# The second mixture's collected head blocks, its last three blocks, shared tail copies and filler products

## The reference

```
x0   cross attention, 8 heads of 128          l1  rotated self attention
x1, x2  cross attention, 16 heads of 8        f2  causal attention, 16 heads of 8, with rotary embedding
m2   mixture of 8 experts on h (1024 x 128), two experts for each token:
     lg  = h @ router                          # 1024 x 8
     w   = softmax(top2(lg))                   # two weights a token, zero for the other experts
     out = sum_e w[:, e] * ((silu(h @ gate_e) * (h @ up_e)) @ down_e)   # hidden size 448
```

## Time and profile before

| | |
|---|---|
| median of 3 runs | 928.2 us (922.79 to 929.34) |
| profiled execution | 926.85 us, its span 925.0 us, so 1.85 us around it |
| PE, DVE, ACT, POOL busy | 861.3, 648.6, 574.3, 305.4 us |
| mean granted clock of PE | 0.988 |
| m2, from the logits to its last table product | 539.6 to 645.4 us of the span |
| chain that ended last, by engine | PE 69%, DVE 14%, ACT 10%, issue 4%, DMA 2% |

### The profile page before, as it was taken

How to read it: one execution, slowest core, us unless ns; L and a number is a source line. 1 busy time by engine, 2 the same in 40 slices (tenths; PEclk the granted TensorE clock), 3 DMA queues, 4 the chain that set the end, 5 groups by cost and what they waited for, 6 DMA issues and landing times.

```text
span 925.0 us, 14478 instructions
## 1 busy us (share of the span) xinstructions
PE 861.3 (93%) x4568; PEld 561.1 (61%) x4568; DVE 648.6 (70%) x1153; ACT 574.3 (62%) x1080; POOL 305.4 (33%) x297
## 2 busy tenths in 40 slices
PE   8999998999899887989899889999999999999997
PEld 4666645775545433535545546776357888888885
DVE  4666716777779578659578663542358999999996
ACT  5456614666557554478578631332677888888886
POOL 0111004764048300028348425435001333444430
PEclk9999999999999999999999999999999999999999
DMA  9000000111000000000000063203008999999882
GB/s 364 14 1 0 0 1 18 52 34 66 1 1 2 1 0 1 1 0 2 2 1 1 3 258 96 82 24 100 7 1 212 241 233 242 245 245 245 234 225 64
DMA packets 27744, 76.70 MB, mean 83 GB/s; under 512 B 4464, under 2 KB 10864, under 8 KB 27264
## 3 DMA queue, kind: packets, MB, share of 16 engines
q1 hardware_dynamic: 26448, 73.50, 28.9%
q0 software_dynamic: 1248, 2.57, 0.8%
HBM read 72.31 MB, written 5.27 MB: 84 GB/s over the span
## 4 chain that ended last, share of the span: by engine, by line
PE 69%; DVE 14%; ACT 10%; issue 4%; DMA 2%; SPq 0%; ACTq 0%; DVEq 0%
PE ps L802 9%; PE ps L804 9%; PE ps L803 9%; PE ps L592 4%; PE ps L1175 4%; PE ps L584 3%; PE ps L603 3%; PE ps L1191 2%; PE ps L219 2%; ACT arena L699 2%; ACT arena L1848 2%; PE ps L1453 2%; PE ps L1534 1%; PE ps L1486 1%; PE ps L1506 1%
## 5 line engine op out<-in xcount | busy, mean ns | idle before, releaser
L802 PE MATMUL ps<-parts 128*128 128x512 f32 x416 | 166.6, 401 | 3.7 <-DVE ps L2463 1.2
L804 PE MATMUL ps<-parts 128*128 128x512 f32 x416 | 162.1, 390 | 0.0
L803 PE MATMUL ps<-parts 128*128 128x512 f32 x416 | 161.9, 389 | 0.0
L832 ACT ACTIVATE parts<-ps 128x512 fp32r<-128x512 f32 x192 | 115.2, 600 | 53.1 <-PE ps L804 24.0
L836 DVE TENSOR_TENSOR parts<-ps,parts 128x512 fp32r<-128x512 f32 x192 | 132.5, 690 | 7.0 <-ACT parts L832 0.8
L820 POOL TENSOR_TENSOR parts<-ring,zeros 128x1024 fp32r<-128x1024 f32 (+2 forms) x36 | 51.1, 1420 | 178.7 <-PE ps L804 141.8
L2463 DVE TENSOR_TENSOR ps<-ps,arena 128x512 f32<-128x512 f32 x156 | 108.1, 693 | 2.7 <-DMA arena<-m_comb 1.8
L802 PEld LDWEIGHTS ps<-parts 128*128 128x128 f32 x416 | 78.2, 188 | 24.6 <-DVE parts L836 3.3
L1997 ACT ACTIVATE ps<-ps 128x512 f32<-128x512 f32 x156 | 90.8, 582 | 2.7 <-PE ps L804 0.4
L804 PEld LDWEIGHTS ps<-parts 128*128 128x128 f32 x416 | 78.1, 188 | 16.4
L803 PEld LDWEIGHTS ps<-parts 128*128 128x128 f32 x416 | 78.1, 188 | 16.2 <-issue 0.5
(11 more groups left out here) (460 smaller groups left out, 1517.8 us busy)
## 6 DMA issues: line engine op xcount, KB each, us to landing
arena<-m_comb SPq DMA_DIRECT2D x156, 256.0 KB, 5.5
ring<-m_in SPq DMA_DIRECT2D x20, 512.0 KB
arena<-m_in SPq DMA_DIRECT2D x4, 1408.0 KB
pack<-pack_in SPq DMA_DIRECT2D x1, 2058.5 KB, 10.6
ring<-m_up_in SPq DMA_DIRECT2D x8, 256.0 KB
slots_x<-empty_in SPq DMA_DIRECT2D x1, 1491.6 KB
pack<-pack_in SPq DMA_DIRECT2D x1, 1186.0 KB, 14.7
pack<-pack_in SPq DMA_DIRECT2D x1, 1149.5 KB, 12.4
```

The costliest lines, as they stand in the source:

```text
L802: nc.tensor.matmul(dst, w_high, x_high, start=start, stop=False, skip_group_check=True)
L803: nc.tensor.matmul(dst, w_high, x_low, start=False, stop=False, skip_group_check=True)
L804: return nc.tensor.matmul(dst, w_low, x_high, start=False, stop=stop, skip_group_check=True)
L832: nc.scalar.activation(m_hh[0:rows, p], ps[0:rows, src, :], ACT.Copy).then_inc(R(t, "_hh"), 1)
```

## The change

- m2's head: `SOON` goes from 6 to 8. The rows are rounded to `s_high` by ACT (an additional copy for each half), POOL subtracts to get `s_low`, and PE multiplies both with 0/1 matrices of 128 x 1024, all in the rounded type F32R: four products of 512 columns for each sequence. Their buffers now lie where `s_xs` is, so SP's row loads wait for the last of these products as well.
- Each row in `slots_x` carries the token's 8 routing weights too (`ROW` from 129 to 137 columns).
- m2's last 3 blocks (`LATE`) are not scattered. From their destinations DVE makes 0/1 matrices of 128 x 1024 (`late_weights` after block 16, `late_place` after blocks 17 to 19); ACT scales and rounds y (`s_yh`), DVE gets the rest (`s_yl`), and PE adds four products of 512 columns for each block to the result's banks, after the loop and ahead of the fills, which are 6 and not 28. Of these three blocks the middle one has bank 4 and not bank 7. The tables are loaded when 20 scatters have landed; the rows of the late pairs read as zero, since `slots_y` is zeroed by one DMA early in the program.
- Attention, last sequence: ACT copies bank 4 and DVE bank 5. Half 1 of the output product is cut in two, 384 columns that wait for 7 sequences and 128 that wait for the last.
- x0: `x_normalise(0, 0)` moves ahead of DVE's six small instructions, with 5 fills on PE ahead of the loop. l1: 6 fills between the two halves of a turn, and 18 where 13 were.
- POOL's `m3_split(0, 0)` waits for the last `down`.

The diff, without the buffers that only get another address and the list of semaphore counts:

```diff
@@ -38,7 +38,8 @@
-SOON = 6
+SOON = 8
+LATE = 3
...
@@ -77,10 +78,10 @@
-ROW = P + 1
+ROW = P + 1 + E
...
-LOADS = (SOON, SOON + 2, SOON + 6, SOON + 12, NB)
-FILL_COUNT, FILL_TABLE = 13, 28
+LOADS = (SOON, SOON + 2, SOON + 6, NB - LATE, NB)
+FILL_COUNT, FILL_TABLE = 13, 6
...
@@ -141,9 +142,17 @@
-        with ExitStack() as overlaid:
-            overlaid.enter_context(nc.sbuf_tensor("below_parts", [P, PARTS], F32))
-            parts = overlaid.enter_context(nc.sbuf_tensor("parts", [P, PARTS_COLS], F32R))
+        def rounded(name, lo, cols):
+
+            with ExitStack() as overlaid:
+                overlaid.enter_context(nc.sbuf_tensor("below_" + name, [P, lo], F32))
+                return overlaid.enter_context(nc.sbuf_tensor(name, [P, cols], F32R))
+
+        parts = rounded("parts", PARTS, PARTS_COLS)
+        places = [rounded(f"places_{b}", lo, SOON * P) for b, lo in enumerate((1408, 6528, 8576, 2432, 3456, 4480, 22912, 26128))]
+        late_places = [rounded("late_0", 24016, T), rounded("late_1", 25040, T), places[0]]
+        late_y = rounded("late_y", 448, 2 * LATE * P)
+        turned_high, turned_low = rounded("turned_high", 20864, T), rounded("turned_low", 21888, T)
...
@@ -588,6 +605,8 @@
                 wait("_pt", w)
+                if w == WAVES - 1:
+                    wait("_last", 1)
...
@@ -595,6 +614,8 @@
                 wait("_pt", 2 * b + 2)
+                if b == B - 1:
+                    wait("_last", 2)
...
@@ -649,9 +670,12 @@
                 residual_seed(pe)
-            for p in range(2):
-                wait("_oT", HB * (p + 1))
-                mm(bank(p), wo, half(a_oT, p), start=rope, stop=True, skip_group_check=True).then_inc(S(done), 1)
+            wait("_oT", HB)
+            mm(bank(0), wo, half(a_oT, 0), start=rope, stop=True, skip_group_check=True).then_inc(S(done), 1)
+            wait("_oT", B - 1)
+            mm(ps[:, 1, 0:HALF - P], wo, a_oT[:, HALF:T - P], start=rope, stop=False, skip_group_check=True)
+            wait("_oT", B)
+            mm(ps[:, 1, HALF - P:HALF], wo, a_oT[:, T - P:T], start=False, stop=True, skip_group_check=True).then_inc(S(done), 1)
...
@@ -696,6 +720,10 @@
                 wait("_turned", w + 1)
+                if b == B - 1:
+                    nc.scalar.activation(a_pt[:, b % 2, NH // 2 * v:NH // 2 * v + 4, :],
+                                         bank(4).rearrange("p (n q) -> p n q", n=4), ACT.Copy).then_inc(R(t, "_pt"), 1)
+                    return
...
@@ -773,8 +801,17 @@
                     inverse(b - 1)
-                if b >= 2:
+                if 2 <= b < B - 1:
                     outputs(b - 2)
+
+            def last_copies(v):
+                wait("_turned", WAVES - 1 + v)
+                nc.vector.tensor_copy(a_pt[:, (B - 1) % 2, NH // 2 * v + 4:NH // 2 * (v + 1), :],
+                                      bank(5).rearrange("p (n q) -> p n q", n=4)).then_inc(R(t, "_last"), 1)
+
+            last_copies(0)
+            outputs(B - 3)
+            last_copies(1)
...
@@ -1088,10 +1125,14 @@
             sp.dma_start(slots_x, empty_in).then_inc(R("m2", "_load1"), 16)
+            sp.wait_ge(S("filled"), 7)
+            sp.dma_start(slots_y[0:2 * T, :].rearrange("(p r c) f -> p r (c f)", p=P, c=2),
+                         zeros[:, :].bitcast(F32).unsqueeze(1).to_broadcast([P, 2 * T // P // 2, 2 * P])).then_inc(R("m2", "_load1"), 16)
...
             sp.wait_ge(S("s_scattered"), 16 * 2 * B)
+            waits(sp, "m2")("_xwl", 2)
...
@@ -1099,7 +1140,7 @@
         def sorted_tables(sp):
-            sp.wait_ge(S("s_out"), 16 * NB)
+            sp.wait_ge(S("s_out"), 16 * (NB - LATE))
...
@@ -1109,6 +1150,12 @@
+        def late(j):
+            return NB - LATE <= j < NB
+
+        def y_bank(j):
+            return 4 if late(j) and (j - (NB - LATE)) % 2 else 7
+
...
@@ -1119,15 +1166,19 @@
             nc.gpsimd.iota(s_dest[:, :, :, P], [[T, 2], [P, B]], channel_multiplier=1).then_inc(R("m2", "_split"), 1)
+            for p in range(2):
+                waits(pool, "m2")("_parts", 3 * p + 2)
+                nc.gpsimd.tensor_tensor(s_low[:, HB * p:HB * (p + 1), :], s_rows[:, 0, HB * p:HB * (p + 1), 0:P],
+                                        s_high[:, HB * p:HB * (p + 1), :], ALU.subtract).then_inc(R("m2", "_split"), 1)
             waits(pool, "m2")("_split", 1)
-            waits(pool, "m2")("_load1", 16)
-            waits(pool, "m2")("_parts", 4)
-            waits(pool, "m2")("_xh", 2)
+            waits(pool, "m2")("_load1", 32)
+            waits(pool, "m2")("_parts", 6)
+            waits(pool, "m2")("_xh", 3)
...
                                                  s_rows[:, k, b, :], None).then_inc(S("s_scattered"), 16)
-            for j in range(NB):
+            for j in range(NB - LATE):
...
@@ -1153,14 +1204,16 @@
             at = [octals[j // 8] // 8 ** (j % 8) % 8 * M2_COLS for j in range(NB)]
-            waits(pe, "m2")("_parts", 4)
+            waits(pe, "m2")("_parts", 6)
+            waits(pe, "m2")("_split", 3)
...
                 waits(pe, "m2")("_pad", b + 1)
-                for lo, hi in ((0, 4), (4, SOON)):
-                    ins = mm(ps[:, 4 + lo // 4, 0:(hi - lo) * P], s_rows[:, 0, b, 0:P], s_places[b][:, lo:hi, :], start=(b == 0), stop=(b == B - 1),
-                             skip_group_check=True)
-                    if b == B - 1:
-                        ins.then_inc(R("m2", "_xwl"), 1)
+                for k, part in enumerate((s_high, s_low)):
+                    for lo, hi in ((0, 4), (4, SOON)):
+                        ins = mm(ps[:, 4 + lo // 4, 0:(hi - lo) * P], part[:, b, :], s_places[b][:, lo:hi, :], start=(b == 0 and k == 0),
+                                 stop=(b == B - 1 and k == 1), skip_group_check=True)
+                        if b == B - 1 and k == 1:
+                            ins.then_inc(R("m2", "_xwl"), 1)
...
@@ -1185,10 +1238,12 @@
                 waits(pe, "m2")("_hl", j + 1)
-                if j >= 1:
+                if late(j - 2):
+                    waits(pe, "m2")("_xh", 4 + j - 2 - (NB - LATE))
+                elif j >= 1 and not late(j - 1):
...
                 for c in range(M2_CH):
-                    ins = mm(ps[:, 7, 0:P], s_hT[0:M2_ROWS, j % 2, c * P:(c + 1) * P],
+                    ins = mm(ps[:, y_bank(j), 0:P], s_hT[0:M2_ROWS, j % 2, c * P:(c + 1) * P],
...
@@ -1204,13 +1259,19 @@
                     down(j - 2)
+            for n in range(LATE):
+                waits(pe, "m2")("_pad", B + 2 + n)
+                waits(pe, "m2")("_xh", 4 + n)
+                for p in range(2):
+                    for k, part in enumerate((s_yh, s_yl)):
+                        mm(bank(p), part[:, n, :], half(late_places[n], p), start=(n == 0 and k == 0), stop=False, skip_group_check=True)
...
                     for k in range(2):
-                        ins = mm(ps[:, p, (b % HB) * P:(b % HB + 1) * P], s_yab[:, k, b, :], s_diag[k][:, b, :], start=(k == 0), stop=(k == 1),
+                        ins = mm(ps[:, p, (b % HB) * P:(b % HB + 1) * P], s_yab[:, k, b, :], s_diag[k][:, b, :], start=False, stop=(k == 1),
...
@@ -1219,9 +1280,8 @@
                 waits(act, "m2")("_xl", p + 1)
-                for k in range(2):
-                    nc.scalar.activation(s_rows[:, k, HB * p:HB * (p + 1), 0:P], bank(4 + p).rearrange("p (b c) -> p b c", b=HB),
-                                         ACT.Copy).then_inc(R("m2", "_parts"), 1)
+                for dst in (s_rows[:, 0, HB * p:HB * (p + 1), 0:P], s_high[:, HB * p:HB * (p + 1), :], s_rows[:, 1, HB * p:HB * (p + 1), 0:P]):
+                    nc.scalar.activation(dst, bank(4 + p).rearrange("p (b c) -> p b c", b=HB), ACT.Copy).then_inc(R("m2", "_parts"), 1)
...
@@ -1238,7 +1298,12 @@
                 waits(act, "m2")("_xw", j + 1)
-                nc.scalar.activation(y_of(j), ps[:, 7, 0:P], ACT.Copy).then_inc(R("m2", "_xwh"), 1)
+                if late(j):
+                    n = j - (NB - LATE)
+                    waits(act, "m2")("_pad", B + 2)
+                    nc.scalar.activation(s_yh[:, n, :], ps[:, y_bank(j), 0:P], ACT.Copy, scale=s_late[:, n:n + 1]).then_inc(R("m2", "_xwh"), 1)
+                else:
+                    nc.scalar.activation(y_of(j), ps[:, y_bank(j), 0:P], ACT.Copy).then_inc(R("m2", "_xwh"), 1)
...
@@ -1274,6 +1339,7 @@
             link(V.tensor_tensor(m_w, m_w, m_d.unsqueeze(2).to_broadcast([P, B, E]), ALU.mult))
+            V.tensor_copy(s_rows[:, :, :, P + 1:ROW], m_w.unsqueeze(1).to_broadcast([P, 2, B, E])).then_inc(R("m2", "_xh"), 1)
...
@@ -1334,13 +1400,44 @@
-            for j in range(NB + 1):
+            def late_weights():
+                waits(dve, "m2")("_c3", 16)
+                link(V.tensor_copy(s_slot, s_to[:, NB - LATE:NB, P]))
+                link(V.tensor_scalar(s_past, s_slot, float(T), float(T), ALU.is_ge, ALU.mult))
+                link(V.tensor_tensor(s_slot, s_slot, s_past, ALU.subtract))
```

(65 more changed lines are left out.)

## The result

The changed kernel takes 915.8 us (median of 4 runs, 912.8 to 918.1) where the kernel before took 928.8 beside it: a ratio of 0.9864, 95% interval 0.9827 to 0.9901. The profiled execution took 912.8, with a span of 910.9; the one of before took 926.85. So the profile lost 14.05 us, where the forecast had 16.3, and the median lost 13.0.

The account below looks back on a forecast made before the run. It took PE's work, clock and waits to bound the kernel. Terms of 2.0 + 1.75 + 4.15 + 3.6 + 0.2 + 4.6 = 16.3 us off the profiled 926.85 gave 910.6, range 906 to 919.

Parts of the forecast that it names:

- What bounds the kernel: Whole kernel: PE's work, clock and waits count; in m2's blocks PE has no gap, so savings beside it don't.
- x0: Start of x0: earlier normalisation and fills keep PE's clock full in turns and scores; -2.0 us, bounds -0.5 and -2.1.
- l1: End of l1: with more fills in PE's waits, layer norm products run at full clock; -1.75 us, bounds 0 and -1.75.
- Tails: Attention tails of x1, x2, f2: shared copies -2.0, cut output product -0.6, x2's clock -1.55; taken -4.15 us.
- clock term of x2: End of x2: `weigh` and `total` at full clock if the shorter waits keep it; another -1.55 us.
- Head: Head of m2: eight sequences by F32R products and DVE comparisons, first block at 561.9; -3.6 us, bounds -3.0 and -4.5.
- Blocks: m2's blocks: two turns fewer on PE, `late_weights` and `late_place` hidden; -0.2 us, bound +1.
- Tail of m2: After m2's last block: late products and fills lead straight to table products; -4.6 us, bounds -3 and -5.9.
- (a): Clock does not follow the fills; l1, x2 and 1.5 of x0 are lost, 4.8 us: 915.4, chance 0.25.
- (b): m2's tail: tables land late, PE idles and returns at half clock; tail +3.5, not -4.6: 918.7, chance 0.08.
- (c): m2's blocks: rows for block 8 come late and PE waits, slower than before: 930 or more, chance 0.02.
- (d): m2's head: F32R products go at the f32 price, head ends 20.4 us behind forecast: 931.0, chance 0.03.

Follow-up runs that it names:

- e_again: The changed kernel once more, word for word, for one profile: 918.8 us (one run).
- e_nofill: The changed kernel with the fills in x0 and l1 as before, DVE's earlier normalisation kept: 916.4 us, ratio 0.9867 to the kernel before.
- e_tails_back: The changed kernel with the attention tails as before (ACT alone makes the last copies, output product in two halves): 916.5 us, ratio 0.9876.
- e_high_only: The changed kernel with m2's head products on the high part alone and POOL's subtractions on one column: 917.5 us (one run).
- e_count28: The changed kernel with 28 fills instead of 13 in m2's head: 913.4 us, ratio 0.9857 to the kernel before.
- e_late0_28: The changed kernel with no late blocks, all 23 scattered, and 28 fills ahead of the table products: 917.0 us, ratio 0.9890.
- e_table0: The changed kernel without the six fills ahead of the table products: 911.3 us, ratio 0.9825 to the kernel before.
- e_best8: The changed kernel with no fills before the table, 28 in the head, and ACT's copies reordered, eight collected blocks: 916.7 us, ratio 0.9875.
- e_soon7: The changed kernel with seven collected blocks instead of eight: 914.5 us, ratio 0.9848 to the kernel before.

## Why the prediction was right, and where its terms were off

The direction, the range and the bulk of the terms held. In the profile 2.2 us are missing: x0 gave 1.95 less than forecast, the other terms 0.8, the start took 0.5 more and m3 0.35, and f1 gave 1.4 that no term had. The median lies 3.0 higher still, and no profile of those executions was kept. e_again shows what such an execution can hold: 5.0 us of a wait in the blocks, 1.5 in x0, 0.8 in the head.

Parts of the gain are shown by runs that take them back: the late blocks (3.9), and the shared copies with the cut product (2.4). The head is read from its steps; no run puts the old head back. What the clock gave (l1 1.6, x2 1.55) rests on one profile of the kernel before; e_nofill bears on the cause in l1 without settling it, and e_tails_back speaks against the one that I gave for x2.

- **What bounds the kernel**: held. In the blocks PE has no gap in the profile after, as before.
- **x0** (-2.0): -1.56 from the turns on, as far as the clock goes, and -0.3 for the reciprocal, which the profiles without a half-clock stretch at 24 show (projections to turns 25.84 against 26.15). -1.86 in such a run. The profiled execution had the stretch at 24 instead, +1.5, so that its x0 gained nothing. That the fills hold the clock in x0 is likely and not shown: x0's first turns are at half clock in both profiles without the fills (before, e_nofill) and in 2 of the 12 with them (e_again, e_high_only).
- **l1** (-1.75): -1.60 measured. Without the fills the stretch came back, but earlier, where it cost 0.5; none of the 12 profiles with the fills has one between 245 and 254. So by the profiles the fills are worth between 0.5 and 1.6, with where the stretch would have fallen; in the medians it doesn't show.
- **Tails** (-4.15): -3.97 measured. The copies (0.6 each in x2 and f2; in x1 a stretch hides them) and the cut product (0.6) are shown by e_tails_back to 0.1 us. The sign that I named for them, PE's idle time before a turn at 0.7, came out at 0.9 (1.2 before). The clock term of x2 (1.54) came, but not by the step that I gave: the half clock stayed away with the old waits too, so that this term was met by luck.
- **Head** (-3.6): -3.33. The step that failed is "two POOL subtractions ... nothing": 0.56 us, because two of DVE's small steps end only when POOL's subtraction does. (The Trainium skill, "SBUF — State Buffer", section "Who interferes with whom", says that a VectorE instruction with two inputs in SBUF and a GpSimd one that reads SBUF block each other, whichever is first, for the whole instruction. The trace agrees for L1341: 0.83 for 0.23. I had weighed no such rule; by it, this term could not be nothing.) The other 0.30 of the 0.86 is for the most part the first comparison, of 1024 columns and not 768, which I had. The scatters too: beside the comparisons one starts 2.27 us after the other, where I had 1.74 at most; that was hidden: SP issues the row loads at 567.29 and PE turns block 8 at 573.40 without a wait. That PE would fall behind at half clock and catch up was right (groups of four products at 1.71, then 0.91; the 1.14 that I named shows only in e_count28). The first block starts 9.8 us before its place, not 11.5: the stretch at 24 (1.8), the 0.5 us at the start and 0.6 less from l1, tails and head, of which f1 gives back 1.4.
- **Blocks** (-0.2): -0.46, as the kernel before also had 0.24 us of waits at `down(1)` and `down(2)`, and nothing of `late_weights` and `late_place` shows in PE.
- **Tail of m2** (-4.6): -4.17; against the forecast `down(22)` starts 0.15 later, and from there to the end of the late products it takes 3.93 and not 3.65; they are 0.231 and not 0.224 each. e_late0_28 gives 3.94 of it to the late blocks. The lower bound (-5.9, "if the fills cost nothing") is e_table0: they cost 1.3, so -5.5.
- **Rivals**: (a) named the measured time, 915.4, and half its mechanism. It had the stretches stay at their places; they moved, to 24 and to others, so that the single terms came and were paid elsewhere. The rule that it takes from the Trainium skill ("TensorE: Matmul & The Clock Gate", section "What's actually happening"), that the clock is judged in windows that run free of the kernel, agrees with e_again: the same program, other places. (b), (c) and (d) didn't occur: no DMA in the tail's chain, no wait at block 8, 0.23 us a product of F32R.
- **The range**: redone from the terms, the summed bounds are 919.7 and 908.2, not 921 and 907.5; the range and the chances don't hang on it.
- **What no term had**: f1's stretch (-1.39 in the profile), m3's +0.35 to +4 when the loads of the routing weights land late, ACT's wait of 3 to 6 us. They differ between profiles at places where no edit was made; the forecast took one favourable execution (926.85 under a median of 928.8) and gave its successor the same luck. The medians' spread shows it: 912.8 to 918.1 for one kernel.

Open: what ACT waits for at its first copy of y. None of the eight experiments on one chip has it, all four on two other chips do. The one profile of the kernel before doesn't have it. Whether it hangs on the chip, and whether the kernel before has it on those chips too, wasn't tried.
Open too: whether the fills or chance keep the clock in x0 and l1. It would take several profiles of each kernel, as one profile of the kernel before can't tell where its stretches usually fall.

## What to carry to other kernels

Judge an edit of 1 to 2 us by the step between two landmarks in the profile, not by the median, when clock stretches of 1.5 us move from run to run. Add fills only where a wait stands anyway, and take them out when the wait goes: the six in front of the table cost 1.3 us. Before work goes to an idle GpSimd, see which small VectorE steps run beside it; "idle engine" isn't "free".

## What the runs showed of the hardware

- VectorE instructions of 0.2 us with two inputs in SBUF ended only with GpSimd's subtraction beside them: 0.83 (changed kernel) and 1.25 us (e_best8); the rounding to bf16 of one input took 0.48, and it too ended with the subtraction. A reciprocal, a reduction and MATCH_REPLACE8 kept their 0.20, 0.22 and 0.15 us beside it.
- The same the other way round, by which comes first: issuing one scatter takes GpSimd 0.96 us. It took 1.96 where it started during one of VectorE's comparisons of 128x1024, and 0.96 to 0.99 where it started just before one (545.53, with the comparison at 545.57). Three of the 16 scatters were slow, and each started two comparisons after the last: 2.27 us apart with comparisons 1.14 apart, 2.00 with those of 128x896, 1.00 apart (e_soon7), 1.74 with those of 128x768, 0.87 apart (before).
- One stretch of half clock cost 1.5 us in x0's turns, 1.7 in its projections, 0.5 in l1's loop (e_nofill), 0.07 in the head, where PE had to wait for others, and nothing at 143; one of twice the length in the head cost 0.84 (e_again).
- The same program on another chip had a 6.1 us wait of ScalarE without a recorded cause (e_again).
